# First three feed-forward elements issued inside the last steps of the first attention; two context loads issued earlier

## The chip, the cores and the metric

The kernel runs on one core of a Trainium2 chip. The metric is the device time of one execution in microseconds (us). The engines are called PE (TensorE, matmuls), DVE (VectorE), ACT (ScalarE), POOL (GpSimd) and SP (SyncE, which here issues most DMAs). Each takes its instructions strictly in the order in which they are written; semaphores make one wait for another.

## The reference

Two decoder layers over 16 batch elements, each of 128 rows by 128 columns (`x`), with a context of 120 rows per element.

```python
x = x + _L0_xattn_ref(_layernorm(x), ctx, ctx, Wq, Wk, Wv, Wo)        # 16 heads of 8, causal, softmax
x = x + _L0_ffn_ref(_layernorm(x), w_up, w_down)                       # 128 -> 512 -> gelu -> 128
x = x + _L1_xattn_ref(_layernorm(x), ctx, ctx, mask, Wq, ...)          # 16 heads of 64, relative positions
x = x + _L1_ffn_ref(_layernorm(x), rhs)                                # int8-like 128x128 product

# inside _L0_ffn_ref, for both weights:
alpha = jnp.mean(jnp.abs(w))
w_t = jnp.sign(w) * (jnp.abs(w) > 0.5 * alpha).astype(w.dtype)
rms = jnp.sqrt(jnp.sum(x * x, axis=-1, keepdims=True)) / jnp.sqrt(d)
x_norm = x / (rms + 1e-8)
```

## The kernel before, in words

The program has three stages, and in each the 16 elements pass one after the other through a software pipeline. `attn0(s, par)` is one step of the first attention, `ffn0(s, par)` one of the feed-forward part (FFN), `layer1(s, par)` one of the second layer. Each engine has its own version of the three functions. In step `s` an engine works on several elements at once: in `attn0(s)` the scores are those of element `s`, the scaling of the probabilities those of `s-1` and `s-2`, the product with the values that of `s-2`, and the residual sum `x_done` that of `s-3`. In `ffn0(s)` DVE takes the statistics of element `s+3` (`bn_stats`, `bn_aggr`, and a sum into `ve`) and normalizes `s+2` into `xn`; POOL takes the root of `s+3` (`rstd`, line 340); PE transposes `xn` of `s+1`, multiplies element `s` with `wup`, transposes the hidden values `hid` of `s-1` and multiplies `hidT` of `s-2` with `wdn`. ACT applies the gelu and copies the transposed values out of PSUM.

`run_steps` sets the order of the steps, the same for every engine: all of attention up to step 16, then `ffn0(-3)`, `attn0(17)`, `ffn0(-2)`, `attn0(18)`, `ffn0(-1)`, `attn0(19)`, and then the FFN from step 0. `attn0(19)` holds nothing. So the first FFN matmul stands behind the last attention matmul on PE. Element 15 is the last: from step 16 on attention has no new scores, and each step holds less.

PSUM has eight banks, `PS[:, 0..7, :]`. Attention keeps its scores in banks 0, 1, 3, 2 (head groups 0, 1, 2, 3), q, k and v in bank 4, the transposed probabilities in 4, 5 and 6, the transposed input in 6, and the outputs in 7. The FFN keeps the transposed input in banks 0 and 1, the `wup` products in 2 and 3, the transposed hidden values in 4 and 5, and the `wdn` products in 6 and 7. It may take a bank only when attention has finished with it; the waits on `A0["probs"]`, `A0["probT0"]` and so on in `ffn0` of PE say so. `probs` counts the exponentials of four head groups per element, so 61 to 64 are those of element 15.

Three small pieces of other work are spread over the attention steps: making `wup` and `wdn` ternary (POOL, lines 332 and 334, in steps 12 to 15), and rounding `rhsT` (DVE, lines 687 to 695), whose transposed form goes through PSUM bank 3 into `qrhs` and `rhs_scale` in step 17 (PE line 1111, DVE lines 743 and 744).

In the third stage `layer1(s)` on SP stores the relative-position products of element `s-1` and `s` (`store`, line 236), reads them back shifted (`shifted`, line 244), and loads context and mask of element `s` (lines 258 and 259). Those of element 0 are loaded in step 0, right after attention's last q, k, v product. Those of element 1 stand in step 1, behind `store(0, 1)` and `shifted(0, 0)`. On PE the key product of element 1 in step 1 waits for that context.

In the tables below a tile's name stands for several things: `relw` is also attention's expanded keys `kexp`, `relr` its second half of `probT0`. Line 964 is the helper `mm`, so it holds nearly all matmuls; line 980 transposes attention's probabilities, 1086, 1131 and 1329 transpose `xn` in the three stages, 1141 transposes `hid`.

## Time and profile before

| | |
|---|---|
| median of 3 runs | 462.59 us (461.73 to 464.74) |
| the profiled execution | 462.21 us |
| its span, first to last instruction | 460.4 us |
| mean granted clock of PE | 0.967 of full speed |
| busy: PE, DVE, ACT, POOL | 93%, 83%, 81%, 55% |

### The profile page before, as it was taken

Reading aid. Unit: us, or ns where it says so; the run is one execution under the profiler, and the core shown is the slowest. Engines: PE = TensorE matmul, PEld = TensorE weight load, DVE = VectorE, ACT = ScalarE, POOL = GpSimd, SP = SyncE. Lnnn points to the kernel's source line nnn. Section 1 sums busy time; section 2 is a strip of 40 time slices with the busy share of each in tenths; the row PEclk is TensorE's granted clock in tenths of the full one; section 3 lists DMA queues with packets and bytes.
Section 4 is the critical chain, followed back from the end, with each engine's and each line's share of the span. In section 5 each row is a group of like instructions: output and inputs, shape, how many; then the busy total and the mean of one; then the engine's idle time right before and its main releaser. Section 6 shows DMA issues by size and latency. Waiting matters only on the chain.

```text
span 460.4 us, 16745 instructions
## 1 busy us (share of the span) xinstructions
PE 428.4 (93%) x6147; PEld 317.8 (69%) x6147; DVE 384.3 (83%) x1316; ACT 370.7 (81%) x1467; POOL 252.8 (55%) x370
## 2 busy tenths in 40 slices
PE   8999999988779989799999999999999999999781
PEld 7556556555547768577887887888788778787570
DVE  5899999998468985489888989989898998988974
ACT  1999999989724564379899899899889989989961
POOL 4488888878935651023244444553654555355684
PEclk9999999999669999899999999999999999999987
DMA  7150000000000002777566565766746766476100
GB/s 216 51 192 22 14 12 6 10 7 8 1 2 1 0 2 69 190 193 186 127 160 150 126 165 123 161 147 140 180 108 159 155 144 163 120 180 148 29 7 23
DMA packets 54392, 44.88 MB, mean 97 GB/s; under 512 B 43952, under 2 KB 49328, under 8 KB 54320
## 3 DMA queue, kind: packets, MB, share of 16 engines
q1 hardware_dynamic: 53616, 43.59, 38.6%
q8 instruction: 46, 0.75, 0.7%
q10 hardware_dynamic: 704, 0.32, 0.2%
q14 instruction: 26, 0.21, 0.2%
HBM read 22.92 MB, written 20.97 MB: 95 GB/s over the span
## 4 chain that ended last, share of the span: by engine, by line
PE 78%; DVE 11%; ACT 4%; POOL 3%; DMA 1%; issue 1%; SPq 1%; POOLq 0%
PE PS L964 68%; PE PS L1161 4%; PE PS L980 2%; PE PS L1141 2%; POOL prob L307 1%; ACT prob L488 1%; DMA ctx<-in_ctxT 1%; DVE relw L709 1%; DVE nmax L666 1%; DVE nmax L668 1%; DVE relr L714 1%; PE PS L1086 1%; DVE nmax L640 1%; DVE qT L699 1%; DVE probT L647 1%
## 5 line engine op out<-in xcount | busy, mean ns | idle before, releaser
L351 POOL TENSOR_TENSOR prob<-prob,rsum 128x480 f32<-128x480 f32 x64 | 62.6, 989 | 70.7 <-DVE rsum L832 37.4
L488 ACT ACTIVATE prob<-prob,nmax 128x120 f32<-128x120 f32 x256 | 100.3, 414 | 0.0
L417 ACT ACTIVATE prob<-PS,nmax 128x120 f32<-128x120 f32 x256 | 89.4, 394 | 3.3 <-DVE nmax L731 2.9
L307 POOL TENSOR_TENSOR prob<-prob,rsum 128x480 f32<-128x480 f32 x64 | 62.5, 986 | 22.1 <-DVE rsum L704 12.4
L417 ACT ACTIVATION_READ_ACCUMULATOR prob<-PS,nmax 128x1 f32 x256 | 61.7, 241 | 0.0
L488 ACT ACTIVATION_READ_ACCUMULATOR prob<-prob,nmax 128x1 f32 x256 | 56.3, 220 | 0.0
L964 PE MATMUL PS<-rT,qv 64*32 64x152 f32 x2048 | 48.1, 297 | 2.4 <-ACT relw L567 2.4
L964 PE MATMUL PS<-ctx,wk 128*128 128x120 f32 x288 | 43.9, 289 | 2.3 <-DMA ctx<-in_ctxT 2.3
L964 PEld LDWEIGHTS PS<-xnT,wq 128*128 128x128 f32 x288 | 36.8, 191 | 9.3 <-issue 6.8
L964 PEld LDWEIGHTS PS<-rT,qv 64*32 64x32 f32 x2048 | 28.6, 106 | 20.6 <-issue 18.6
L964 PE MATMUL PS<-xnT,wq 128*128 128x128 f32 x288 | 42.5, 285 | 0.0
L964 PEld LDWEIGHTS PS<-ctx,wk 128*128 128x128 f32 x288 | 36.6, 195 | 7.1 <-issue 3.6
L964 PE MATMUL PS<-probT,hv 120*64 120x128 f32 x512 | 35.9, 284 | 3.3 <-ACT probT L595 3.3
L964 PE MATMUL PS<-wv,ctx 128*120 128x512 f32 (+1 forms) x96 | 39.0, 487 | 0.0
L964 PE MATMUL PS<-kT,qu 64*128 64x120 f32 x512 | 36.2, 281 | 0.0
L964 PE MATMUL PS<-relw,qT 32*128 32x480 f32 x128 | 34.4, 613 | 0.4 <-DVE relw L709 0.4
L964 PE MATMUL PS<-wo,oT_pairs 128*128 128x128 f32 x256 | 34.8, 280 | 0.0
L964 PEld LDWEIGHTS PS<-probT,hv 120*64 120x64 f32 x512 | 28.0, 139 | 7.9 <-ACT probT L595 3.7
L964 PEld LDWEIGHTS PS<-wo,oT_pairs 128*128 128x128 f32 x256 | 31.8, 195 | 1.8 <-ACT fin L502 0.8
L964 PEld LDWEIGHTS PS<-kT,qu 64*128 64x128 f32 x512 | 31.1, 188 | 2.5 <-issue 1.7
L980 PEld LDWEIGHTS PS<-ident,prob 64*120 64x120 f32 x512 | 18.9, 143 | 19.2 <-issue 19.2
L386 POOL TENSOR_TENSOR rstd_o<-ve_o,mhalf 128x1 f32<-128x1 f32 x16 | 13.1, 820 | 28.0 <-DVE ve_o L899 28.0
(195 smaller groups left out, 1100.6 us busy)
## 6 DMA issues: line engine op xcount, KB each, us to landing
rel_scratch<-relw SPq DMA_DIRECT2D x128, 152.0 KB, 2.7
relr<-rel_scratch SPq DMA_DIRECT2D x64, 240.0 KB, 4.3
ctx<-in_ctxT SPq DMA_DIRECT2D x32, 60.0 KB, 1.9
out_x<-fin SPq DMA_DIRECT2D x16, 64.0 KB, 2.2
x_all<-in_x SPq DMA_DIRECT2D x1, 640.0 KB, 7.1
wr<-in_wr SPq DMA_DIRECT2D x1, 512.0 KB, 5.0
wq<-in_wq SPq DMA_DIRECT2D x1, 512.0 KB, 3.7
wk<-in_wk SPq DMA_DIRECT2D x1, 512.0 KB, 4.5
```

Of the source, the lines that this page charges most:

```text
L307: return pool.tensor_tensor(pr, pr, cols(rsum[p], g, HG).unsqueeze(2).to_broadcast([S, HG, SK]), ALU.mult)
L351: return pool.tensor_tensor(pr, pr, cols(rsum[p], g, HG).unsqueeze(2).to_broadcast([S, HG, SK]), ALU.mult)
L386: pool.tensor_tensor(rstd2[p][:, :], ve2[p][:, :], mhalf[:, :], ALU.pow).then_inc(A1["orstd"], 1)
L417: last = act.activation(cols(prob[p], n, SK), cols(scores, q, SK), ACT.Exp, bias=nmax[p][:, n:n + 1], accum_out=ssum[p][:, n:n + 1])
L488: last = act.activation(cols(pr, n, SK), cols(pr, n, SK), ACT.Exp, bias=bias[:, n:n + 1], accum_out=total[:, n:n + 1])
L640: dve.tensor_reduce(out=cols(nmax[p], 2, HG), in_=heads(PS[:, 3, 0:HG * SK], HG), op=ALU.max, axis=AX.X, negate=True).then_inc(A0["nmax"], 1)
L647: dve.tensor_copy(query_half(probT0[0], 1), heads(PS[0:SK, 5, :], 2 * HG)).then_inc(A0["probT1"], 1)
L666: dve.tensor_reduce(out=cols(nmax[p], 0, HG), in_=heads(PS[:, 0, 0:HG * SK], HG), op=ALU.max, axis=AX.X, negate=True).then_inc(A0["nmax"], 1)
L964: return pe.matmul(o, a, b, start=start, stop=stop)
L980: last = pe.transpose(PS[0:SK, bank, q * S // 2:(q + 1) * S // 2], cols(prob[p], g * HG + q, SK)[rows], ident_sb[rows, rows])
L1141: last = pe.transpose(PS[:, 4 + p, c * S:(c + 1) * S], cols(hid[p], c, D), ident_sb[:, :])
L1161: last = pe.transpose(PS[0:SK, bank, q * S // 2:(q + 1) * S // 2], cols(prob[p], g * HG + q, SK)[rows], ident_sb[rows, rows])
```

## The change

Each engine gets a function `crossing()`, which writes out in what order it takes `attn0(14)` to `attn0(18)` and `ffn0(-3)` to `ffn0(2)`, and no longer the same for all. The last head group's and second head group's score banks change places (1 and 2), as do banks 5 and 6, through all of attention. The rounded `rhsT` passes through bank 7 in step 15, beside the output of element 12. POOL's last addition into `wdn` moves from step 15 to step 17. ACT loads the gelu table at the end of step 16. The FFN's waits for free banks follow the new numbers. Context and mask of elements 0 and 1 of the third stage are loaded one after the other as soon as attention's last q, k, v product is done.

```diff
@@ run_steps
-            peeled(attn0, LOOPS[0][1], NB + 1)
-            for s in range(3):
-                peeled(ffn0, s - 3, s - 2)
-                peeled(attn0, NB + 1 + s, NB + 2 + s)
-            peeled(ffn0, 0, LOOPS[1][0])
+            peeled(attn0, LOOPS[0][1], NB - 2)
+            crossing()
+            peeled(ffn0, 3, LOOPS[1][0])
@@ SP
+            def load_context(t, p):
+                at, mask_at = held(sp, t * SK), held(sp, t * S * SK)
+                sp.dma_start(ctx_sb[p][:, :], ctxT[:, bass.ds(at, SK)]).then_inc(A1[f"ctx_loaded{p}"], 16)
+                sp.dma_start(mask_sb[p][:, :], bass.AP(mask.tensor, mask_at, [[SK, S], [1, SK]]))\
+                    .then_inc(A1[f"mask_loaded{p}"], 16)
@@ SP layer1
-                    if isinstance(t, int) and t < 2:
-                        sp.wait_ge(A0["qkv_ps"], NB)
-                    after(sp, A1["hv_ps"], 2 * t - 2)
...
+                    if not (isinstance(t, int) and t < 2):
+                        sp.wait_ge(A1["hv_ps"], 2 * t - 2)
+                        load_context(t, p)
@@ SP ffn0
+                if at_step(s, -3):
+                    sp.wait_ge(A0["qkv_ps"], NB)
+                    for t in range(2):
+                        load_context(t, t)
@@ POOL
-                    if at_step(s, 13 + 2 * k):
+                    if at_step(s, 13 + 4 * k):
                         link(pool.tensor_tensor(w[:, :], w[:, :], change, ALU.add))
+            def crossing():
+                attn0(14, 0)
+                ffn0(-3, 1)
+                attn0(15, 1)
+                ffn0(-2, 0)
+                attn0(16, 0)
+                attn0(17, 1)
+                ffn0(-1, 1)
+                attn0(18, 0)
+                ffn0(0, 0)
+                ffn0(1, 1)
+                ffn0(2, 0)
@@ PE
+            def crossing():
+                attn0(14, 0)
+                attn0(15, 1)
+                ffn0(-3, 1)
+                ffn0(-2, 0)
+                ffn0(-1, 1)
+                attn0(16, 0)
+                ffn0(0, 0)
+                attn0(17, 1)
+                ffn0(1, 1)
+                attn0(18, 0)
+                ffn0(2, 0)
@@ DVE attn0, before the residual sum of element s - 3
+                    if at_step(s, NB - 1):
+                        link(dve.tensor_copy(qrhs[:, :], PS[:, 7, D:2 * D]))
+                        link(dve.tensor_copy(rhs_scale[:, :], PS[:, 7, 2 * D:3 * D]))
@@ PE attn0, before the output product of element s - 3
+                    if at_step(s, NB - 1):
+                        pe.wait_ge(setup_v, 17)
+                        pe.transpose(PS[:, 7, D:2 * D], qx[0][:, :], ident_sb[:, :]).then_inc(setup_p, 1)
+                        mm(PS[:, 7, 2 * D:3 * D], fin[0][:, :], ident_sb[:, :]).then_inc(setup_p, 1)
@@ PE ffn0, waits for free banks
-                        pe.wait_ge(A0["probs"], 63)
+                        pe.wait_ge(A0["probs"], 62)
                     if at_step(s, 1):
-                        pe.wait_ge(setup_v, 19)
+                        pe.wait_ge(A0["probs"], 64)
```

In the same notation the other two compute engines take their steps so. DVE: `ffn0(-3)`, `attn0(14)`, `attn0(15)`, `ffn0(-2)`, `attn0(16)`, `ffn0(-1)`, `attn0(17)`, `ffn0(0)`, `attn0(18)`, `ffn0(1)`, `ffn0(2)`. ACT: `attn0(14)`, `attn0(15)`, `attn0(16)`, `ffn0(-3)`, `ffn0(-2)`, `ffn0(-1)`, `attn0(17)`, `ffn0(0)`, `attn0(18)`, `ffn0(1)`, `ffn0(2)`. SP takes all five attention steps first.

PE before, from element 15's second product with the values (`relr,vexp`) to the third `wup` product:

```order
L964 MATMUL PS<-relr,vexp 32x128 x8
L1111 MATMUL PS<-ident,qx 128x128
L964 MATMUL PS<-ident,fin 128x128
L964 MATMUL PS<-wo,oT 128x128
L1131 MATMUL PS<-ident,xn 128x128
L964 MATMUL PS<-wup,xnT 128x512
L1131 MATMUL PS<-ident,xn 128x128
L964 MATMUL PS<-wup,xnT 128x512
L1131 MATMUL PS<-ident,xn 128x128
L1141 MATMUL PS<-ident,hid 128x128 x4
L964 MATMUL PS<-wup,xnT 128x512
```

Now, the same engine, from the first transposed probabilities of element 15 (line 1035 is 980 of before, 1019 is 964, 1185 is 1131, 1195 is 1141):

```order
L1035 MATMUL PS<-ident,prob 120x64 x16
L1019 MATMUL PS<-wup,xnT 128x512
L1185 MATMUL PS<-ident,xn 128x128
L1019 MATMUL PS<-wo,oT 128x128
L1035 MATMUL PS<-ident,prob 120x64 x16
L1019 MATMUL PS<-probT,vexp 32x128 x8
L1019 MATMUL PS<-relr,vexp 32x128 x8
L1019 MATMUL PS<-wup,xnT 128x512
L1185 MATMUL PS<-ident,xn 128x128
L1195 MATMUL PS<-ident,hid 128x128 x4
L1019 MATMUL PS<-wo,oT 128x128
L1019 MATMUL PS<-wup,xnT 128x512
```

The first `wup` product now stands before the second half of element 15's probabilities, the second one before the last attention product (`wo,oT`), and the two products for `rhsT` are gone from here.

POOL before, steps 15 to 17 and the FFN's first roots (`prob` rows are scalings, `vexp` spreads the values, `rstd` is the FFN's root):

```order
L315 TENSOR_TENSOR vexp<-v,vmask 120x512
L307 TENSOR_TENSOR prob<-prob,rsum 128x480 x3
L334 TENSOR_TENSOR wdn<-wdn,relw 128x512
L307 TENSOR_TENSOR prob<-prob,rsum 128x480
L315 TENSOR_TENSOR vexp<-v,vmask 120x512
L307 TENSOR_TENSOR prob<-prob,rsum 128x480 x3
L340 TENSOR_TENSOR rstd<-ve,half 128x2
L307 TENSOR_TENSOR prob<-prob,rsum 128x480
L340 TENSOR_TENSOR rstd<-ve,half 128x2 x3
```

POOL now, from the root of element 0 on:

```order
L357 TENSOR_TENSOR rstd<-ve,half 128x2
L324 TENSOR_TENSOR prob<-prob,rsum 128x480
L332 TENSOR_TENSOR vexp<-v,vmask 120x512
L324 TENSOR_TENSOR prob<-prob,rsum 128x480 x3
L357 TENSOR_TENSOR rstd<-ve,half 128x2
L324 TENSOR_TENSOR prob<-prob,rsum 128x480
L332 TENSOR_TENSOR vexp<-v,vmask 120x512
L324 TENSOR_TENSOR prob<-prob,rsum 128x480 x4
L351 TENSOR_TENSOR wdn<-wdn,relw 128x512
L357 TENSOR_TENSOR rstd<-ve,half 128x2 x2
```

Two roots have moved ahead of the last scalings, and the addition into `wdn` behind them.

SP before, at the start of the third stage:

```order
L258 DMA ctx<-in_ctxT 128x120
L259 DMA mask<-in_mask 128x120
L236 DMA rel_scratch<-relw 32x1216 x8
L244 DMA relr<-rel_scratch 64x8x120 x2
L258 DMA ctx<-in_ctxT 128x120
L259 DMA mask<-in_mask 128x120
L244 DMA relr<-rel_scratch 64x8x120 x2
```

SP now:

```order
L232 DMA ctx<-in_ctxT 128x120
L233 DMA mask<-in_mask 128x120
L232 DMA ctx<-in_ctxT 128x120
L233 DMA mask<-in_mask 128x120
L99 UNCONDITIONAL_BRANCH
L99 REGISTER_ALU
L99 COMPARE_AND_BRANCH
L253 DMA rel_scratch<-relw 32x1216 x8
L261 DMA relr<-rel_scratch 64x8x120 x4
```

The second context and mask stand ahead of all stores, and the four shifted reads follow one another.

## Rows read from the trace of the kernel before

**Rows 1.** Windows: busy time by engine, then granted clock (PEclk), DMA share, GB/s.
```profile
core 0: us, PE busy (x) PEld busy (x) DVE busy (x) ACT busy (x) POOL busy (x), PEclk, DMA share, GB/s
142.00:170.00 28.00, 28.00 (x186) 21.68 (x184) 24.82 (x137) 15.40 (x38) 16.57 (x22) 1.00 0.00 1
191.27:430.00 238.73, 237.05 (x4014) 189.09 (x4016) 211.19 (x655) 212.96 (x785) 109.98 (x176) 0.99 0.63 150
```

**Rows 2.** Timeline of PE over the crossing: start, length, what [idle before].
```profile
120.02 1.11 PE L980 MATMUL PS<-ident,prob 64*120 64x64 f32 x16 [1.89 <-POOL prob L307]
...
126.00 1.11 PE L980 MATMUL PS<-ident,prob 64*120 64x64 f32 x16 [0.92 <-POOL prob L307]
...
127.98 1.08 PE L964 MATMUL PS<-relr,vexp 120*32 120x128 f32 x16
...
131.60 0.30 PE L1131 MATMUL PS<-ident,xn 128*128 128x128 f32 x1 [1.48 <-DVE xn L770]
...
141.10 1.02 PE L964 MATMUL PS<-wup,xnT 128*128 128x512 f32 x2
141.96 0.27 PE L1131 MATMUL PS<-ident,xn 128*128 128x128 f32 x1
...
142.51 1.06 PE L964 MATMUL PS<-wdn,hidT 128*128 128x128 f32 x8
143.40 1.02 PE L964 MATMUL PS<-wup,xnT 128*128 128x512 f32 x2
```

**Rows 3.** Windows of half a microsecond in which the granted clock changes.
```profile
119.50:120.00 0.50, 0.00 (x0) 0.01 (x1) 0.14 (x1) 0.50 (x4) 0.50 (x2) 0.54 0.00 0
...
129.50:130.00 0.50, 0.50 (x4) 0.43 (x3) 0.07 (x1) 0.00 (x0) 0.00 (x0) 0.72 0.00 0
...
133.00:133.50 0.50, 0.50 (x3) 0.11 (x1) 0.41 (x3) 0.00 (x0) 0.01 (x1) 0.70 0.00 0
...
140.00:140.50 0.50, 0.50 (x6) 0.50 (x5) 0.32 (x1) 0.41 (x3) 0.40 (x1) 0.98 0.00 0
```

**Rows 4.** Timeline of POOL, steps 15 to 17.
```profile
117.54 1.27 POOL L334 TENSOR_TENSOR wdn<-wdn,relw 128x512 f32<-128x512 f32 x1
118.89 0.98 POOL L307 TENSOR_TENSOR prob<-prob,rsum 128x480 f32<-128x480 f32 x1
...
121.06 2.88 POOL L307 TENSOR_TENSOR prob<-prob,rsum 128x480 f32<-128x480 f32 x3
124.20 0.71 POOL L340 TENSOR_TENSOR rstd<-ve,half 128x2 f32<-128x2 f32 x1 [0.26 <-DVE ve L774]
```

**Rows 5.** Timeline of DVE: steps 14 and 15, then the FFN's first statistics.
```profile
105.79 0.66 DVE L666 TENSOR_REDUCE nmax<-PS 128x4 f32<-128x480 f32 x1 [0.62 <-PE PS L964]
...
117.08 0.29 DVE L740 COPY oT<-PS 128x128 f32<-128x128 f32 x1
...
123.35 0.28 DVE L759 BATCH_NORM_STATS2 stat<-x_all 128x6 f32<-128x128 f32 x1
...
123.89 0.23 DVE L774 TENSOR_SCALAR ve<-eps,mv 128x2 f32<-128x2 f32 x1
```

**Rows 6.** Timeline of DVE and POOL in the third stage, where two of them overlap.
```profile
210.49 1.93 POOL L351 TENSOR_TENSOR prob<-prob,rsum 128x480 f32<-128x480 f32 x2 [3.97 <-DVE rsum L832]
...
210.59 0.97 DVE L853 TENSOR_SCALAR xn<-x_all,mv,rstd 128x128 f32<-128x128 f32 x1
```

**Rows 7.** Timeline of SP, PE and DVE around the second context, third stage.
```profile
184.48 1.35 SPq L244 DMA_DIRECT2D relr<-rel_scratch  x2
185.88 0.62 SPq L258 DMA_DIRECT2D ctx<-in_ctxT  x1
...
191.27 2.06 PE L964 MATMUL PS<-ctx,wk 128*128 128x120 f32 x8 [2.30 <-DMA ctx<-in_ctxT]
191.56 0.65 DVE L920 TENSOR_TENSOR prob<-PS,relr 128x480 f32<-128x480 f32 x1
...
193.47 1.26 PE L964 MATMUL PS<-rT,qv 64*32 64x152 f32 x32
...
194.67 1.15 PE L964 MATMUL PS<-ctx,wk 128*128 128x120 f32 x8
```

125 lines of the change are left out of this document (74 added, 51 removed).

## The prediction

> **What bounds the kernel now.** I read the busy shares by stretch first, then PE's own timeline, then what it waits for. In the FFN, from 142 us on, PE is busy for 28.00 of 28.00 us, and in the third stage from 191.27 to 430 us for 237.05 of 238.73 us [rows 1]. In both, DVE, ACT and POOL have time left. So whatever brings PE earlier to one of these stretches should come out at the end in full, and nothing that only relieves another engine there counts. The places where PE is not the bound are the seams between the stages. At the first seam the last attention product with the values ends at 127.98 + 1.08 = 129.06 us, and the fourth `wup` product, from which the FFN runs in its regular step, starts at 141.10 [rows 2]. Those 12.04 us hold the two products for `rhsT`, one output product, an idle 1.48 us before the first transpose of the FFN [rows 2], and three FFN steps that begin from an empty pipeline. They also hold slow matmuls: the granted clock falls from 2.4 to 1.2 GHz at 119.5 us, after PE had waited 1.89 us for POOL [rows 2, 3], comes back at 129.8, falls again at 133.2 after the waits at the FFN's start, and is back at 140.0 [rows 3]. At the second seam, PE waits 2.30 us for the context of element 1 of the third stage and then runs its product at the low clock: 2.06 us against 1.15 for the same eight instructions at 194.67 [rows 7].
>
> **Part 1, the price: what the FFN's early pieces cost attention.** Ahead of step 14, DVE now takes the statistics of element 0. Before they last from 123.35 to 123.89 + 0.23, so 0.77 us [rows 5]. DVE has an idle 0.62 in that step, in which it waits for PE's scores [rows 5]; some 0.15 us is left over. POOL then has the root of element 0 before step 15: 0.71 us in its row [rows 4], 0.67 to the start of the next operation. POOL is busy without a gap there, so step 15 runs some 0.8 late on POOL, on the transposes that wait for it, and on DVE, where element 13's `oT` (117.08 to 117.37 before [rows 5]) ends at about 118.1. After it DVE has `ffn0(-2)`: den, statistics of element 1, `xn` of element 0, `ve`. From the statistics' 0.77 and the four operations between them I put this at 1.0 us, so `ve` is there at 119.1, and POOL's root of element 1 ends at 119.1 + 0.7 = 119.8. The scaling of element 14 that PE waits for begins then; before it began at 118.89 [rows 4]. The addition into `wdn`, 1.27 us ahead of it [rows 4], has gone from this place, and the net is still **0.9 us late**, since POOL now waits for DVE. From there POOL has the same sequence: one scaling, `vexp`, three scalings (to 121.06 + 2.88 = 123.94 before [rows 4]), now to 124.8. The last scaling of element 15 follows at once, where before the root at 124.20 [rows 4] stood between; it begins at 124.8, as late as before.
>
> On ACT the exponentials of element 15 that need DVE's last maximum come behind `ffn0(-2)`, some 1.3 us later than before. They are done by about 121.8, and POOL's scaling that needs them begins at 123.9: cover of 2 us. The gelu table load follows behind the copy of element 14's second half, and after it ACT has the transposed input of element 0 by 124.4. Nothing but the first `wup` product waits for it.
>
> PE, with its clock low as before: the second of POOL's three scalings ends two thirds into their 2.88 us, at 123.0 before [rows 4] and at 123.9 now, so the transposes of element 15's first half run from 124.0 to 125.1. Then comes the first `wup` product: 0.86 us at the high clock (141.10 to 141.96 [rows 2]), so some 1.8 at the low one, to 126.9. Transpose of element 1 and output product of element 14 reach 127.4, and the transposes that began at 126.00 before [rows 2] begin at 127.4. The last product with the values therefore ends at 127.4 + 3.06 = 130.4 us and not 129.06: the length 3.06 is that from 126.00 to 129.06. So the first piece of the FFN does delay attention's end, by **1.3 us**.
>
> **Part 1, the return.** What stands between that end and the fourth `wup` product is then: `wup` of element 1 (0.86), the transpose of `xn` and four of `hid` (141.96 to 142.51, 0.55), one output product (0.2, a quarter of the four products with `wdn`), `wup` of element 2 (0.86), 0.55 again, and the first product with `wdn` (142.51 to 143.40, 0.89) [rows 2]. That is 3.91 us at the high clock. To it I add 0.3 for ACT's copy that the third `wup` needs and 0.4 for DVE's `xn` of element 3, which stands behind the residual sum of element 15. Gelu of element 0 runs on ACT while PE is still in attention's last products. The fourth `wup` starts at 130.4 + 4.6 = 135.0 us, where before it started at 141.10: **6.1 us saved**. The clock is the large unknown in it. PE is now without a gap from about 124.0 on. Before, it took from 126.00 to 129.8 of gap-free work until the clock was back the first time, and the second time it came back at 140.0 [rows 2, 3], after a longer stretch of work. So I take it to be up by 130. If it comes up only where attention's end and half of the early FFN steps have passed, those 3.91 us double to at most 7.8, and 3.0 are left of the 6.1. If it never falls, because PE's wait for POOL is cut by the transpose of element 0, POOL's 124.8 is still the bound, PE's 3.06 and 1.8 us shrink by about a half, 2.4 together, and the saving is 8.5.
>
> The two products for `rhsT` and their DVE copies move to step 15. PE pays some 0.3 there, DVE 0.6 in front of a wait for PE like that of step 14; POOL, by then 0.8 late, hides both. The exchange of banks 1 and 2 and of 5 and 6 renames both sides of each wait, so I cost it at nothing from start to end of attention. The waits of the FFN for free banks ask for exponentials that are done by 121.8, before any of its `wup` products. The `wdn` addition ends at 127.0 on POOL, 7 us before its first use.
>
> **A rule that could add to the price.** In the trace, a normalization of DVE that takes its input and puts its output in SBUF begins just behind a POOL scaling and takes 0.97 us, until the first of the two POOL operations has ended [rows 6]. The Trainium skill, "SBUF — State Buffer", section "Who interferes with whom", says that VectorE and GpSimd share a pair of ports, which one takes for a whole instruction while the other stands still; by this rule the trace agrees. In the crossing DVE's `xn` of element 1 would meet a scaling of POOL at 124.8. It could last 0.97 us as well and end at 125.8, and PE needs it at 126.9, so it is covered. The `ve` of element 0 would meet POOL's addition into `wup` in step 14; were it held for most of such an addition (1.27 us in its row), step 14 would be some 0.7 us later on DVE, and the saving 5.4 instead of 6.1. The row of a `ve` at 123.89, begun under a scaling, has 0.23 us [rows 5, 4], so I take the price as nothing.
>
> **Part 2, the early context.** The wait of 2.30 us goes. What is late next: PE's key product of element 1 runs at 188.97 to 189.9, then a transpose to 190.2, and the relative products that follow ask for DVE's sum `added0` of element 0. That sum waits for the shifted read issued at 184.48, ahead of the context in SP's queue [rows 7], so it isn't earlier than before: 191.56 + 0.6 = 192.15 [rows 7]. Those products start at 192.15 and not at 193.47 [rows 7], 1.3 us earlier. At the high clock their end, 192.9, stands against 194.67 [rows 7]: 1.8 at most. If the clock falls again in the 1.95 us wait that is left, and comes back at the same place as before, the work that now runs ahead of the wait is worth about 0.7; if it falls later, nothing is left (0.1). PE's similar wait of 1.89 us was followed by a fall [rows 2, 3], so I take **0.7**, with 0 and 1.8 as ends. SP issues two DMAs fewer at 185.88, but the next shifted read waits for its stores.
>
> **The sum.** 462.21 - 6.1 - 0.7 = 455.4 us for the profiled execution. The median of the runs before is 0.4 above the profiled one, so I forecast **455.7 us**, 1.5% less. A measurement of this kernel can tell about 1% from no change.
>
> **The rivals.**
> 1. *The clock stays low through the early FFN.* Saving 3.0 + 0.1: 459.5. For it: PE's work from 124 on is interleaved with waits for four engines, and the clock took until 140.0 the second time. Against it: those waits are shorter than the ones before.
> 2. *The clock does not fall, or comes back before 127.* Saving 8.5 + 1.8: 452.3. For it: PE's longest wait has a transpose and a product in it. Against it: 1.5 us and more of it remain, and 1.89 were enough [rows 2].
> 3. *The overlap is mostly hidden.* The early FFN pieces lie in front of attention's on each in-order queue. If two of the three put PE a further 2 us behind, 6.1 becomes 2.1: 459.8 with part 2.
> 4. *Slower: a convoy.* Each engine mixes the steps in another order, so an FFN piece may wait for an attention piece of another engine that itself waits for an FFN piece. One such round trip, from DVE's statistics over POOL, DVE, PE and ACT to the `wup` product, takes about 3 us by the trace: 129.06 to 131.60 up to the transpose [rows 2], and a copy on ACT. With three of them, one per element, the end of attention would be 9 later: 462.6 + 9 - 6.8 = 464.8. It decides the sign once attention's last product ends after 137.2 us (130.4 + 6.8).
> 5. *The early context does nothing*, since the shifted read holds PE as long: 456.5. It lies within the forecast's range.
>
> **How the numbers follow.** Forecast, with either end of part 2 and 1.5 us of error in part 1: 0.66. Rival 2: 0.12. Rival 1: 0.10. Rival 3: 0.08. Rival 4: 0.04. The range is 451.8 to 459.9: it takes in rivals 2 and 1 nearly at their numbers, and leaves out rival 4 and the far halves of 2 and 3. Faster by over 1% means under 458.0: nearly all of the forecast and rival 2, 0.76. Within 1%: rivals 1 and 3 and a rest of the forecast, 0.20. Slower by over 1%: 0.04.
>
> **What the changed kernel's profile would show.** The POOL scaling of element 14 in step 16 begins near 119.8; attention's last product with the values ends near 130.4; the fourth `wup` starts near 135; between the two PE has no idle stretch over half a microsecond, and the granted clock is 1.00. The regular FFN step stays at 2.30 us (141.10 to 143.40 [rows 2]). In the third stage no wait for `ctx` is left, and one for `added0` of about 2 us stands in its place. The forecast is wrong if the last product ends much later than 131, if the clock falls again behind it, or if the third stage gives back what it got because DVE or the DMAs come as late as before.

## The result, and the profile after

| | before | changed kernel |
|---|---|---|
| median of the runs | 462.16 us (461.36 to 464.74, 4 runs) | 457.34 us (456.54 to 459.7, 4 runs) |
| profiled execution: time, span, granted clock | 462.21, 460.4, 0.967 | 456.54, 454.7, 0.985 |

The ratio is 0.9864, with a 95% interval of 0.9822 to 0.9906: faster by 1.4%, where 1.5% was forecast. Ratios leave out executions that a lower clock made over 1.5% longer than the fastest of their kernel; of the changed versions that is one (594.66 us at a clock of 0.653, experiment 9). Of the 5.7 us between the two profiled executions I account for each below. At the fourth `wup` product the changed kernel leads by 7.2 us, at the end of the FFN by 6.5, behind the second seam by 7.5, at the end by 5.7.

**The crossing.** The timeline of PE in the changed kernel, as [rows 2]:

```profile
117.43 0.64 PE L1019 MATMUL PS<-relr,vexp 120*32 120x128 f32 x16
...
121.22 0.68 PE L1035 MATMUL PS<-ident,prob 64*120 64x64 f32 x16 [1.28 <-POOL prob L324]
...
124.47 0.69 PE L1035 MATMUL PS<-ident,prob 64*120 64x64 f32 x16 [1.04 <-POOL prob L324]
125.08 1.13 PE L1019 MATMUL PS<-wup,xnT 128*128 128x512 f32 x2
...
128.38 0.64 PE L1019 MATMUL PS<-relr,vexp 120*32 120x128 f32 x16 [0.30 <-DVE relr L760]
128.96 1.12 PE L1019 MATMUL PS<-wup,xnT 128*128 128x512 f32 x2
...
133.91 1.02 PE L1019 MATMUL PS<-wup,xnT 128*128 128x512 f32 x2
```

The transposes of element 15's first half and the first `wup` stand behind one another at 124.47 and 125.08. The last product with the values begins at 128.38 and ends at 129.0, where it ended at 129.06 before. The fourth `wup` begins at 133.91 and not at 141.10. From the product at 117.43, which stands in attention's step 15, that is 16.48 us. The same product before is this row, and from it the way took 24.73 us:

```profile
116.37 0.65 PE L964 MATMUL PS<-relr,vexp 120*32 120x128 f32 x16
```

The 1.13 us of a `wup` is what it takes at the high clock (1.23 at 132.36 before), while before one took 2.05 to 2.07. The windows say the same: the granted clock is 1.00 from 117 to 142 us, in this window as in the others, where [rows 3] has 0.54 at 119.5.

```profile
122.00:124.00 2.00, 1.12 (x32) 0.61 (x24) 1.24 (x5) 1.97 (x5) 2.00 (x3) 1.00 0.03 8
```

The timeline of POOL answers to [rows 4], then three rows of DVE to [rows 5] and [rows 6]:

```profile
103.78 1.27 POOL L351 TENSOR_TENSOR wup<-wup,hsq 128x512 f32<-128x512 f32 x1
...
119.43 0.70 POOL L357 TENSOR_TENSOR rstd<-ve,half 128x2 f32<-128x2 f32 x1 [0.78 <-DVE ve L816]
120.09 0.99 POOL L324 TENSOR_TENSOR prob<-prob,rsum 128x480 f32<-128x480 f32 x1
...
122.27 3.83 POOL L324 TENSOR_TENSOR prob<-prob,rsum 128x480 f32<-128x480 f32 x4
```

```profile
104.32 0.77 DVE L816 TENSOR_SCALAR ve<-eps,mv 128x2 f32<-128x2 f32 x1
...
124.23 1.00 DVE L812 TENSOR_SCALAR xn<-x_all,mv,tiny 128x128 f32<-128x128 f32 x1
125.16 0.97 DVE L816 TENSOR_SCALAR ve<-eps,mv 128x2 f32<-128x2 f32 x1
```

The scaling of element 14 begins at 120.09, 1.2 us later than before. The `ve` of element 0 takes 0.77 us instead of 0.22 and ends at 105.09, within 0.04 us of POOL's addition into `wup` (103.78 + 1.27).

**The FFN.** PE is again busy for the whole of a window of 28 us, but compare the counts with [rows 1]: 181 matmuls, where there were 186.

```profile
134.50:162.50 28.00, 28.00 (x181) 20.76 (x180) 25.43 (x140) 15.44 (x37) 18.13 (x24) 1.00 0.00 0
```

```profile
143.16 1.02 PE L1019 MATMUL PS<-wup,xnT 128*128 128x512 f32 x2
144.18 0.33 PE L1185 MATMUL PS<-ident,xn 128*128 128x128 f32 x1
...
145.68 1.02 PE L1019 MATMUL PS<-wup,xnT 128*128 128x512 f32 x2
146.54 0.27 PE L1185 MATMUL PS<-ident,xn 128*128 128x128 f32 x1
...
147.98 1.02 PE L1019 MATMUL PS<-wup,xnT 128*128 128x512 f32 x2
```

A step takes 2.52 us (143.16 to 145.68), the next 2.30 (to 147.98), together 4.82. The loop's first pair of steps takes 4.65, the other three 4.80 to 4.82, where before each took 4.60: 0.67 us in all. In the long ones the transpose of `xn` begins 1.02 us behind `wup` instead of 0.86. What it waits for is DVE. In these rows of DVE, `xn` begins 0.27 us behind the small MEMSET ahead of it in one step and 0.07 in the next:

```profile
143.51 0.06 DVE L656 MEMSET gap<- 128x1 f32 x1
143.78 0.35 DVE L812 TENSOR_SCALAR xn<-x_all,mv,tiny 128x128 f32 x1
...
145.99 0.06 DVE L656 MEMSET gap<- 128x1 f32 x1
146.06 0.33 DVE L812 TENSOR_SCALAR xn<-x_all,mv,tiny 128x128 f32 x1
```

**The second seam.** The chain of waits (start, length, what), against [rows 7]:

```profile
177.96 0.65 SPq L261
...
178.66 6.37 DMA relr<-rel_scratch
...
185.78 0.58 DVE prob L975
...
186.49 9.14 PE PS L1019 x156
...
195.65 0.42 ACT relw L609
```

No wait for `ctx` is left, and the relative products wait for DVE's sums with the shifted read. From the first shifted read's issue to ACT's copy it takes 17.69 us; before it took 18.67 (184.48 to 203.15). The granted clock stays at 1.00 there, where before it was at 0.50 from 191.2 to 194.6. Experiment 2 asks whether the early context or the clock made the difference.

**The tail.** Windows of before, then of the changed kernel (PEclk is the third number from the end):

```profile
434.00:437.00 3.00, 1.32 (x27) 0.88 (x23) 2.89 (x11) 3.00 (x13) 2.58 (x6) 1.00 0.07 22
437.00:440.00 3.00, 2.80 (x20) 2.47 (x21) 2.84 (x10) 3.00 (x15) 2.52 (x4) 0.50 0.00 0
440.00:443.00 3.00, 2.96 (x37) 2.55 (x38) 2.22 (x12) 2.25 (x8) 2.61 (x5) 0.93 0.00 0
```

```profile
428.00:431.00 3.00, 1.47 (x17) 0.95 (x17) 2.93 (x9) 3.00 (x13) 2.17 (x4) 0.92 0.07 22
431.00:434.00 3.00, 2.55 (x18) 2.33 (x20) 2.76 (x13) 2.39 (x12) 2.61 (x6) 0.50 0.00 0
434.00:437.00 3.00, 3.00 (x25) 2.57 (x23) 0.74 (x6) 1.36 (x3) 2.92 (x6) 0.50 0.02 5
```

The clock falls in both, but for some 3.4 us before (437.0 to 440.4) and 6.8 in the changed kernel (430.5 to 437.3). From the same group of transposes (419.00 before, 411.50 after) to POOL's last sum (457.93 and 452.22) it takes 38.93 and 40.72 us:

```profile
419.00 0.68 PE L1161 MATMUL PS<-ident,prob 64*120 64x64 f32 x16
```

```profile
411.50 0.68 PE L1229 MATMUL PS<-ident,prob 64*120 64x64 f32 x16
```

That is the 1.8 us by which the lead shrinks at the end.

### The profile page after: what moved, and what is told of

The parts are those of the page before. It is cut to its first block, busy times and chain, and to the rows that moved or that the text cites. A ratio compares the mean times of both kernels' runs of the same rounds, so it can differ in the third digit from the quotient of the medians.

```text
span 454.7 us, 16744 instructions
## 1 busy us (share of the span) xinstructions
PE 422.3 (93%) x6147; PEld 313.4 (69%) x6147; DVE 385.8 (85%) x1316; ACT 371.5 (82%) x1467; POOL 253.9 (56%) x370
## 4 chain that ended last, share of the span: by engine, by line
PE 77%; DVE 13%; ACT 4%; POOL 2%; DMA 1%; issue 1%; SPq 0%; POOLq 0%; DVEq 0%
PE PS L1019 67%; PE PS L1229 4%; PE PS L1035 3%; ACT prob L531 2%; PE PS L1195 1%; DMA relr<-rel_scratch 1%; DVE relr L760 1%; DVE nmax L712 1%; DVE nmax L714 1%; DVE relw L755 1%; POOL prob L324 1%; DVE nmax L683 1%; DVE probT L690 1%; PE PS L1145 1%; DVE nmax L777 1%
## 5 line engine op out<-in xcount | busy, mean ns | idle before, releaser
L1019 PE MATMUL PS<-ctx,wk 128*128 128x120 f32 x288 | 42.9, 285 | 0.0
L1019 PE MATMUL PS<-wo,oT_pairs 128*128 128x128 f32 x256 | 36.0, 287 | 0.5 <-ACT fin L545 0.5
L1019 PEld LDWEIGHTS PS<-wo,oT_pairs 128*128 128x128 f32 x256 | 32.8, 200 | 2.4 <-ACT fin L545 1.3
L1035 PEld LDWEIGHTS PS<-ident,prob 64*120 64x120 f32 x512 | 17.8, 135 | 19.0 <-issue 19.0
```

The source lines that it names most:

```text
L1019: return pe.matmul(o, a, b, start=start, stop=stop)
L1035: last = pe.transpose(PS[0:SK, bank, q * S // 2:(q + 1) * S // 2], cols(prob[p], g * HG + q, SK)[rows], ident_sb[rows, rows])
```

## The experiments

Each was timed beside the kernel before on its chip; ratios are to it. The stretches of all profiled executions first, since most verdicts rest on them. **Crossing** is from the start of the product with the values in attention's step 15 to the start of the fourth `wup`; **FFN** from there to SP's first shifted read. PEclk says whether the granted clock fell between 117 and 133 us. "Kept busy" stands for constant products on PE, "one read first" for a changed order of two DMAs; both are explained below.

| kernel | crossing | PEclk | FFN | time us (median) | ratio [95%] |
|---|---|---|---|---|---|
| before | 24.73 | falls | 43.38 | | |
| changed | 16.48 | 1.00 | 44.05 | 457.34 | 0.9864 [0.9822, 0.9906] |
| changed, again | 16.48 | 1.00 | 44.06 | 458.19 | 0.9857 [0.9806, 0.9909] |
| crossing alone | 18.22 | falls | 44.05 | 458.45 | 0.9859 [0.9810, 0.9907] |
| context alone | 24.60 | falls | 43.38 | 464.68 | 0.9994 [0.9959, 1.0029] |
| FFN unrolled | 18.23 | falls | 43.38 | 459.99 | 0.9895 [0.9839, 0.9952] |
| before, kept busy | 21.33 | 1.00 | 43.86 | 458.91 | 0.9897 [0.9840, 0.9953] |
| `wdn` addition in step 15 | 18.94 | falls | 44.06 | 458.85 | 0.9906 [0.9870, 0.9943] |
| one read first | 18.03 | falls | 44.05 | 456.39 | 0.9863 [0.9810, 0.9915] |
| third stage kept busy | 17.86 | falls | 44.04 | 456.37 | 0.9849 [0.9804, 0.9894] |
| `wup` addition in step 12 | 16.46 | 1.00 | 44.06 | 461.50 | 0.9932 [0.9892, 0.9971] |
| kept busy, FFN unrolled | 16.47 | 1.00 | 43.39 | 455.57 | 0.9822 [0.9770, 0.9874] |
| the same, again | 16.48 | 1.00 | 43.37 | 454.35 | 0.9778 [0.9730, 0.9827] |
| the same, one read first | 16.47 | 1.00 | 43.38 | 456.41 | 0.9809 [0.9753, 0.9865] |

The rest of the same executions: **third stage** from the first shifted read to the group of transposes with which the tail begins (419.00 before), with whether the clock fell at the second seam; **tail** from there to POOL's last sum, with how long the clock was low in its first low stretch. A later one, up to the end, they all have.

| kernel | contexts | third stage | clock at the seam | tail | low in it |
|---|---|---|---|---|---|
| before | late | 234.52 | falls | 38.93 | 3.4 |
| before, kept busy | late | 232.67 | 1.00 | 39.00 | 3.4 |
| crossing alone | late | 234.25 | falls | 40.73 | 6.8 |
| context alone | early | 234.52 | falls | 39.58 | 3.4 |
| changed | early | 233.54 | 1.00 | 40.72 | 6.8 |
| changed, again | early | 232.90 | 1.00 | 39.51 | 3.4 |
| FFN unrolled | early | 234.86 | falls | 41.36 | 6.8 |
| `wdn` addition in step 15 | early | 232.53 | 1.00 | 39.72 | 3.4 |
| one read first | early | 232.85 | 1.00 | 39.60 | 3.4 |
| third stage kept busy | early | 233.18 | 1.00 | 39.27 | 0 |
| `wup` addition in step 12 | early | 235.47 | falls | 39.59 | 3.4 |
| kept busy, FFN unrolled | early | 233.14 | 1.00 | 39.48 | 0 |
| the same, again | early | 233.53 | 1.00 | 39.45 | 0 |
| the same, one read first | early | 235.28 | falls | 39.25 | 0 |

**1. The crossing alone.** The changed kernel with only element 0's context loaded early:

```
-                    if not (isinstance(t, int) and t < 2):
-                        sp.wait_ge(A1["hv_ps"], 2 * t - 2)
+                    if not (isinstance(t, int) and t < 1):
+                        after(sp, A1["hv_ps"], 2 * t - 2)
                         load_context(t, p)
...
-                    for t in range(2):
-                        load_context(t, t)
+                    load_context(0, 0)
```

> The changed kernel without its second part: the context of element 1 of the third stage is again loaded in step 1, behind the shifted read. Theory (the two parts add up): the fourth wup product starts at about 134 us as in the changed kernel (133.9 there, 141.1 before), PE waits for the context again (about 2.3 us), and the time is 0.5 to 1 us above the changed kernel's, 4.5 to 6 below before. Rival (the early context gives nothing, since the shifted read holds PE as long): the time is that of the changed kernel.

The time is that of the changed kernel within the intervals: 0.9859 against 0.9864. PE waits 1.28 us at 122.16 as in the changed kernel, but here the clock falls behind that wait:

```profile
122.00:124.00 2.00, 1.54 (x40) 1.26 (x44) 0.95 (x3) 1.98 (x9) 2.00 (x3) 0.83 0.04 8
128.00:130.00 2.00, 2.00 (x20) 1.46 (x18) 0.29 (x1) 0.00 (x0) 0.95 (x2) 0.50 0.00 0
```

So one and the same order of instructions in the crossing has two outcomes, 16.48 us and 18.22. Of the eight profiled executions with this crossing and no added products in it (two of them with one of POOL's additions in another step), the clock stayed up in three.

**2. The context alone.** The kernel before with the first two contexts loaded early, nothing else.

```
...
             def ffn0(s, par):
-                pass
+                if at_step(s, -3):
+                    sp.wait_ge(A0["qkv_ps"], NB)
+                    for t in range(2):
+                        load_context(t, t)
```

> The kernel before with the early contexts alone. Theory: the crossing is as before (fourth wup at about 141), no wait for the context, a wait of PE for DVE's sum in its place, the relative products 1.0 us earlier than before counted from the end of the FFN, time 0.5 to 1.5 us under before. The shifted read of element 0 lands 0.5 us or more later after its issue than before (5.2 us from the end of its issue before, 5.8 in the changed kernel), since the next one is now issued right behind it. Rival (the later landing in the changed kernel has another cause, such as the shift of everything by 7 us): it lands as before, and the gain is 1.5 us or more.

No difference can be measured (0.9994). In the trace the stretch of relative and key products begins 7.84 us after the first shifted read's issue (186.84 to 194.68) instead of 9.06 (184.48 to 193.54). This is 1.2 us earlier, but it is not what the lost wait gives: with the late contexts, and PE's waits for them of 2.02 and 0.88 us still there, the same stretch begins 7.87 us after the issue in experiment 1 (180.64 to 188.51) and 7.72 in experiment 4, whose chain of waits has

```profile
188.61 1.15 PE PS L964 x8
...
189.87 9.08 PE PS L964 x156
```

The 9.06 were those of one execution, in which the context came late and its product ran at the low clock (2.06 us instead of 1.15). In experiment 2 the clock falls at 196.0, and the whole third stage takes 234.52 us, as before. The second table sorts by the clock and not by the contexts: where it stayed up at the seam, 232.67 us with late contexts and 232.53 to 233.54 with early ones; where it fell, 234.25 and 234.52 with late, 234.52 to 235.47 with early. No gain from the early contexts shows, neither in the time nor in a trace, though late contexts at the high clock were profiled only once.

**3. The FFN unrolled.** The changed kernel with the eight looped FFN steps written out:

```
             peeled(ffn0, 3, LOOPS[1][0])
-            looped(ffn0, LOOPS[1])
-            peeled(ffn0, LOOPS[1][1], NB - 1)
+            peeled(ffn0, LOOPS[1][0], NB - 1)
```

> The changed kernel with its FFN written out from step 4 to 14 instead of a loop over pairs of steps. In the changed kernel the steps of the loop take 2.40 us and not 2.30, and the lead of 7.2 us at the fourth wup is 6.5 at the end of the FFN. Theory (DVE with the loop's extra instructions needs 4.80 us for a pair, and is now the bound, since it no longer has the head start it had before): the steps take 2.30 us, the lead stays 7.1 to 7.2, the time is about 0.6 us under the changed kernel. Rival (DVE needs 2.4 us for a step with or without the loop, because of its port shared with POOL): nothing changes.

```profile
135.39 1.02 PE L1018 MATMUL PS<-wup,xnT 128*128 128x512 f32 x2
...
137.69 1.02 PE L1018 MATMUL PS<-wup,xnT 128*128 128x512 f32 x2
```

Every step takes 2.30 us, and the FFN stretch 43.38 instead of 44.05. So in the traces the looped form costs 0.67 us once PE has no slack ahead of it; the runs that have the loop written out (here and in experiment 9) all take 43.37 to 43.39, the others with this crossing 44.04 to 44.06. The loop was unrolled on every engine, and that DVE's part is what counts is read from the rows above. The time doesn't show the gain (0.9895): in the profiled execution the clock fell at the crossing, at the second seam and in the tail, and against the changed kernel's execution the crossing takes 1.75 us more, the third stage 1.32 and the tail 0.64.

**4. The kernel before, kept busy.** Nineteen constant products on PE in the waits of the old crossing, results unused:

```
+                    if isinstance(s, int) and s >= NB:
+                        pe.wait_ge(A0["probs"], 61)
+                        for _ in range({16: 7, 17: 3, 18: 6}[s]):
+                            mm(PS[:, 0, 0:D], mean_w[:, :], mean_w[:, :])
...
+                    if at_step(s, 0):
+                        pe.wait_ge(setup_v, 19)
+                        for _ in range(3):
+                            mm(PS[:, 3, 0:D], mean_w[:, :], mean_w[:, :])
```

> The kernel before with 19 products of a constant on PE, whose results nobody reads, in its idle stretches between 118 and 135 us: 7 in step 16, 3 in step 17, 6 in step 18, 3 behind the first wup product. It computes all that before does. Theory (a good part of the crossing's saving is the clock, which no longer falls): the granted clock stays at 1.00 from 117 to 142, and the fourth wup starts about 3 to 4.5 us earlier than 141.1, at 137 or so, the time 3 to 4 under before. Rival (the saving is overlap, and the clock has little part in it): the fourth wup is earlier by under 1.5 us though the clock stays up. If the clock falls all the same, this tells nothing about either.

```profile
128.01 0.64 PE L964 MATMUL PS<-relr,vexp 120*32 120x128 f32 x16 [0.30 <-DVE relr L714]
...
131.61 1.10 PE L964 MATMUL PS<-wup,xnT 128*128 128x512 f32 x2 [0.46 <-ACT xnT L472]
...
138.29 1.02 PE L964 MATMUL PS<-wup,xnT 128*128 128x512 f32 x2
```

The old order at a clock of 1.00 has the fourth `wup` at 138.29 us, 2.8 earlier than [rows 2], and the time falls by 1.0%. This splits the gain. At the high clock the crossing takes 21.33 us in the old order and 16.48 in the new: 4.85 us are overlap. At a clock that falls it is 24.73 against 17.86 to 18.23: 6.5 to 6.9. The low clock costs the old order 3.4 us and the new one 1.4 to 1.75. A small part of the 21.33 is the added products' own: `xn` of element 1 is ready at 132.53, and its transpose begins at 133.21, behind the three products that follow the first `wup`. So, as an estimate from these rows, the overlap is worth up to 0.6 us less than 4.85 and the clock as much more. What in the new order gave it (the FFN's early pieces, the banks, the moved `rhsT`) no run separates, but for the `wdn` addition of experiment 5.

The time is a warning: 0.9897 [0.9840, 0.9953] can't be told from the 0.9864 of the changed kernel or the 0.9859 of experiment 1. Nineteen added products gave nearly as much as the whole new order. In this execution the clock also stayed up at the second seam, which before it did not.

**5. The `wdn` addition back in step 15.** `13 + 4 * k` becomes `13 + 2 * k` in the changed kernel.

> The changed kernel with one edit: GpSimd's addition into wdn stands in step 15 again instead of step 17. Theory (GpSimd's chain of scalings sets when the last probabilities are transposed, and with them everything up to the fourth product with wup): GpSimd is idle for 0.78 us ahead of the root at 119.43, and the addition takes 1.35, so the last scaling of element 14 and the transposes behind it come about 0.6 us later (transposes at 121.8 instead of 121.22, last product with values at about 129.0 instead of 128.38). In exchange nothing of 1.35 us stands ahead of the third element's root, which may give up to 0.3 back at the wait of 0.34 ahead of the transpose at 132.41: the fourth product with wup at 133.9 to 134.6, time 0 to +0.6 us against the changed kernel, ratio to before about 0.987. Rival (the vector engine sets the crossing, GpSimd only waits for it): the transposes stay at 121.2 and nothing moves. Rival 2 (a later start leaves TensorE idle longer, 1.9 instead of 1.28 us, and its clock falls there): the fourth product at 136 to 137, time +2 to +3.

```profile
118.80 1.26 POOL L351 TENSOR_TENSOR wdn<-wdn,relw 128x512 f32<-128x512 f32 x1
...
121.11 0.98 POOL L324 TENSOR_TENSOR prob<-prob,rsum 128x480 f32<-128x480 f32 x1
```

The crossing is 0.7 to 1.1 us longer than in the others whose clock fell. The theory said 0.6 for the start of the transposes (they begin at 122.24, 4.61 after the product with the values, against 3.79 in the changed kernel: 0.8), and a part back at the third root, of which nothing shows. Moving this addition was worth some 0.8 us in the trace; the time (0.9906 [0.9870, 0.9943]) can't be told from the changed kernel's.

**6. One read first.** In the changed kernel, SP issues element 0's second shifted read when the first has landed:

```
                     sp.wait_ge(A1["stored1"], 64 * t + 64)
+                    if at_step(t, 0):
+                        sp.wait_ge(A1["relr00"], 32)
                     shifted(t, p, 1)
```

> The changed kernel, in which SyncE issues the second shifted read of element 0's relative scores only when the first has landed. In the changed kernel all four reads are issued within 4.2 us from 177.96 on and the one waited for lands at 185.1, 7.2 us after the issue began; before it was 6.5. Theory A (reads issued back to back share the DMA engines, and the early contexts, by letting SyncE issue them sooner, made the first one slower): the first read lands about 0.5 to 0.7 us earlier (6.5 after the issue of the first), the second some 2 to 4 us later, and the wait of the relative products moves to the second: ahead of the next softmax step ACT's copies come up to 2 us later unless they have that slack. Time -0.5 to +2 us against the changed kernel. Theory B (the landing is the DMA's own latency of some 6.4 us from the issue, whatever else is queued): first read unchanged, second later, time 0 to +2 us.

The chain has `180.46 4.92` for the landing, 5.6 us after the issue began at 179.77. Without the edit, it is 6.1 to 7.3 us in nine executions where four reads are issued in a row. This agrees with theory A's first half and doesn't show it: the changed kernel alone has 7.1 and 6.4 in its two executions, and in experiment 9 a read issued alone took 6.0. The next context then waits in SP's queue until 194.22 and PE for it until 198.26. The time is 456.39: no loss, and no gain that the intervals can tell.

**7. Third stage kept busy.** The changed kernel with constant products in waits of the third stage:

```
+                    if at_step(s, NB + 2):
+                        keep_busy(1, 2)
...
+                    if at_step(s, NB + 2):
+                        keep_busy(7, 3)
...
+                    if at_step(t, 1):
+                        keep_busy(3, 10)
                     after(pe, A1["added0"], t)
...
+                    if isinstance(s, int) and s >= NB + 1:
+                        keep_busy(1, 4)
                     pe.wait_ge(A1["probT3"], t + 1)
```

> The changed kernel with constant products on TensorE in idle time of the third stage alone: ten ahead of the wait for the relative scores at 183.7 to 186.5, and in steps 17 and 18 four ahead of the last product with values, two and three ahead of the output product and the dequantising product of step 18. Their results are not used. Theory (the lead of 7.5 us at 411.57 shrank to 5.7 at the end because the granted clock fell at 430.8 for 6.4 us in the changed kernel and at 437.0 for 3.2 us before it): with the clock at 1.00 from 425 to 438 the stretch from the transposes at 411.57 to the end takes about 2 us less (43.1 us now), and the whole about 455 us, ratio to before 0.981 to 0.984; at the second seam nothing changes where the clock did not fall (up to 1.5 us in the executions where it did). Rival (the tail is set by the chain ScalarE-VectorE of the last softmax and dequantisation, where TensorE's speed is hidden): clock 1.00 there but the stretch from 411.57 to the end stays 43 us, time unchanged. Rival 2 (the products themselves delay the waits they stand ahead of by more than they give): +0.5 us or more.

```profile
431.00:434.00 3.00, 2.35 (x32) 1.98 (x30) 2.79 (x11) 3.00 (x16) 2.61 (x6) 1.00 0.02 5
434.00:437.00 3.00, 2.96 (x52) 2.50 (x49) 1.97 (x13) 1.76 (x6) 2.61 (x5) 1.00 0.00 0
```

The clock is 1.00 up to 443, and the tail takes 39.27 us (412.21 to 451.48) instead of 40.72. Of the 2 us expected, 1.45 came. But most of it comes without the products too: in the changed kernel's other profiled execution (experiment 9) the clock was low for 3.4 us there and not 6.8, and the tail took 39.51. The two products ahead of the output product stand behind the wait there (they start at 432.16, when it has ended) and hold it up by 0.55 themselves: a small share of rival 2. All six runs lie between 455.8 and 458.1.

**8. The `wup` addition in step 12.** `13 + 4 * k` becomes `12 + 5 * k`: a test of what held the `ve` of element 0.

> The changed kernel with GpSimd's addition into wup in step 12 instead of step 13. Theory (the variance row of FFN element 0 takes 0.77 us on the vector engine instead of 0.2 because GpSimd's addition runs over it, and this delays every later step of the attention by 0.5): that row takes 0.20 to 0.25, the span from the copy of oT ahead of it to the copy of oT(13) falls from 14.57 to about 14.0, and the time by 0.5 us. Rival (GpSimd then works 1.27 us longer ahead of step 13's scalings, which the transposes wait for): the row is short but oT(13) comes no earlier, or up to 1.3 us later; time 0 to +1.3. Rival 2 (the row is long for a reason of its own, such as its operands): it stays at 0.77.

```profile
97.15 1.26 POOL L351 TENSOR_TENSOR wup<-wup,hsq 128x512 f32<-128x512 f32 x1
...
106.59 1.27 POOL L332 TENSOR_TENSOR vexp<-v,vmask 120x512 f32<-120x512 f32 x1 [1.26 <-PE PS L1019]
```

```profile
99.62 0.69 PE L1035 MATMUL PS<-ident,prob 64*120 64x64 f32 x16 [2.02 <-POOL prob L324]
```

```profile
107.30 0.59 DVE L816 TENSOR_SCALAR ve<-eps,mv 128x2 f32<-128x2 f32 x1
```

My theory's cure was worse than the harm. PE waits 2.02 us for POOL at 99.62, its clock falls and is low from 100.8 to 114.5, and attention reaches step 15's product with the values at 122.23 instead of 117.43. The row itself speaks for the mechanism all the same: `ve` now meets another POOL operation, `vexp`, and ends with it (107.89 and 107.86), taking 0.59 instead of 0.77. So it is as long as what is left of POOL's operation. What the 0.5 us are worth to the whole wasn't measured.

**9. Kept busy, and the FFN unrolled.** Experiments 7 and 3 together, and four constant products in each of the two waits for POOL in step 16:

```
+                    if at_step(s, NB):
+                        keep_busy(5, 4)
                     pe.wait_ge(A0["probT1"], free)
...
                     freed(pe, (A0["v"], free, t + 2), (A0["probT0"], t, t - 1))
+                    if at_step(s, NB):
+                        keep_busy(4, 4)
```

> The kernel before it in this list, with two more edits: constant products in the two stretches of 1.28 and 1.04 us where TensorE waits for GpSimd's scalings in step 16 of the crossing (four each), and the eight FFN steps of the loop written out one after another instead of looped. Theory: the clock stays at 1.00 through the crossing in every execution (the fourth product with wup at 133.9 in the profile, where the runs with a low clock had 135.4 and 136.6), each FFN step takes 2.30 us instead of 2.40 (0.7 us over the stage), and the third stage as in the kernel before it. Together about 454 us in the median, ratio to before 0.977 to 0.982, with less spread between executions than the changed kernel. Rival (written-out steps cost as much in fetched code as the loop cost on the vector engine): FFN steps of 2.30 in the trace but no gain beyond 455. Rival 2 (the clock falls elsewhere as soon as it is held in one place): the low stretches come back at other places and the time is 456 to 457, as the changed kernel.

Five of its six executions lie between 454.05 and 456.46 us. The crossing takes 16.47 and the FFN 43.39. The rerun beside the changed kernel:

> The kernel with the clock held and the FFN unrolled again, beside the changed kernel and the one with one read first. Theory: median 454 to 456, below the changed kernel by 1.5 to 2.5 us, ratio to before 0.979 to 0.983. Rival (its lead over the changed kernel came from executions with a lucky clock): within 1 us of the changed kernel.

It gave 454.35 us, with all six between 454.15 and 454.94, where the changed kernel's six lie between 454.64 and 459.1:

> The changed kernel as it stands, so that it is timed beside the others on one chip. Expected 456.5 to 458, ratio to before 0.984 to 0.988. In the trace the stretch from the value product of step 15 to the fourth product with wup takes 16.5 us if the granted clock stays at 1.00 there and 18.0 to 18.3 if it falls; the stretch from there to the first shifted read takes 44.05 either way.

So in this set the version does every time what the changed kernel did at its best; in the first set it did so in three of these five. The medians differ by 3.8 us, where 1.5 to 2.5 were expected. Its interval, 0.973 to 0.983, is the lowest of the study. With one read first on top:

> The kernel with the clock held and the FFN unrolled, with the edit of the one read first on top: SyncE issues element 0's second shifted read when the first has landed. Theory (a read issued alone lands 5.6 us after its issue began, one with three more behind it 6.1 to 7.2, and the relative products wait for the first only): the first read lands at most 5.7 us after its issue began, and the third group of relative copies comes 0.5 to 0.7 us earlier; the time is 0.3 to 0.7 us under that of the kernel without the edit, which runs again beside it. Rival (that landing differs by as much from execution to execution, and the second read becomes the one waited for): the same time within 0.3 us.

The median was 456.41 (0.9809), no gain, and the six lie between 454.33 and 458.73: the steadiness is gone. The first read lands 6.0 us after its issue began, but PE then waits 0.79 for the next context, and in the profiled execution the clock fell behind that wait (199.7 to 203.1). This execution was also some 2.6 us late before the crossing began (120.06 against 117.33 to 117.55), with the clock low between 21 and 29 us, so not all of its 458.73 belongs to the edit. The expected 5.7 was missed, the gain was absent.

## Why the prediction was right, and where it was wrong

**The time** (455.7 forecast, 457.34 measured, within the range) came out near, and some of that is luck. Part 1 gave about 1 us more than forecast because the clock happened to stay up, part 2 was credited with 0.7 us that no run shows, and two losses for which the sum had no term (the FFN's loop and the tail) took away 2.5.

**Part 1, the price.** `ve` of element 1 was put as done at 119.1; it begins at 119.12 and ends at 119.34. The scaling of element 14 was put at 119.8 and begins at 120.09, which is 1.2 late instead of 0.9. I put the extra down to the port rule that I weighed and priced at nothing; no run took the hold away, so its price is argued. The `ve` of element 0 took 0.77 us while POOL's addition ran, and experiment 8 shows its length follow POOL's operation. By the Trainium skill, "SBUF — State Buffer", section "Who interferes with whom", one of the two stands still for the other's whole instruction; the trace agrees with it here. My row against it was the wrong witness: that `ve` of 0.23 began at 123.89, 0.05 us before the scaling ended at 123.94 [rows 4, 5], so there was nothing left to hold it. In the changed kernel `xn` at 124.23 and `ve` at 125.16 took 1.00 and 0.97, both under scalings. As forecast, these two were covered.

**Part 1, the clock.** The step "PE, with its clock low as before" failed in the profiled execution: the clock never fell, which is rival 2's condition, with 0.12 as its chance, and came in three of eight executions. With it the last product ended at 129.0 and not 130.4, and the fourth `wup` came at 133.91 and not 135.0. The sum itself was good: in the four variants with this order whose clock fell in the profiled execution (experiments 1, 3, 6, 7) it came at 134.99 to 136.59. Rival 2's bonus of 2.4 us was too large: the low clock costs the new order 1.4 to 1.75. What was wrong was to give the two clocks fixed chances for the kernel, when they are two outcomes of executions.

**"Whatever brings PE earlier to one of these stretches should come out at the end in full"** was the step that failed on substance, together with "the regular FFN step stays at 2.30". Busy for 28.00 of 28.00 hid that DVE's looped step took as long: before, DVE takes 2.33 and 2.49 us for two steps in turn, 4.82 for PE's 4.60:

```profile
146.51 0.21 DVE L752 TENSOR_SCALAR tiny<-rstd 128x1 f32<-128x1 f32 x1
...
148.84 0.21 DVE L752 TENSOR_SCALAR tiny<-rstd 128x1 f32<-128x1 f32 x1
...
151.33 0.21 DVE L752 TENSOR_SCALAR tiny<-rstd 128x1 f32<-128x1 f32 x1
```

It drew on a head start from PE's late start: its `xn` of element 4 was done at 139.49, and PE took it at 141.96. In the changed kernel it is done at 134.56 and taken at 134.77, and from 143.16 on PE followed DVE, a pair of steps in 4.80 to 4.82. Experiment 3 gives the 0.67 us back, and in experiment 4, where PE came 2.8 us earlier in the old order, half a microsecond of it is lost already (43.86).

**Part 2** was put at 0.7 with 0 and 1.8 as ends; the two profiled executions differ by 0.98, and that is not its return. In the runs it comes out at the lower end, as rival 5 had it: alone it is 0.9994 [0.9959, 1.0029], experiment 1 without it is level with the changed kernel, and the third stage is as long with late contexts as with early ones once the clock did the same (experiment 2). The step that failed is that the products would start 1.3 us earlier, at 7.67 us after the shifted read's issue. They started 8.53 after it in the changed kernel and 7.88 in its other execution, while the late contexts reached 7.72 and 7.87 (experiments 4 and 1). There too DVE's sum was done only 7.52 and 7.43 us after the issue, so the wait for the context hid next to nothing but that sum. The price of 1.3 us was read from one execution, with its 9.06 (experiment 2). The `added0` wait was forecast as about 2 us and is 2.85 in one execution of the changed kernel and 2.21 in the other; in the first the shifted read took 0.64 us longer to land, for a reason that isn't shown.

**The tail** had no term in my sum. The 1.8 us lost there go with how long the clock is low there, and I find no edit that they belong to: executions with the new crossing have 3.4 us and 6.8, those with the old one, of which there are three, 3.4. With constant products it isn't, and the tail is 1.45 shorter (experiment 7); with 3.4 us of low clock instead of 6.8 the same kernel's is 1.21 shorter. In sum: 7.19 - 0.67 + 0.98 - 1.79 = 5.71 us of 5.67 measured. This adds up two executions and not the edits: the last two terms are different in the changed kernel's other one.

Rivals 3 and 4 didn't occur: attention's end moved by less than 0.1 us (129.06 to 129.02), and to 130.11 to 130.84 in experiments 3, 6 and 7, at the low clock for which 130.4 was forecast, and no engine waited in a round. What stays open is why the clock falls in one execution and not in another with the same waits; no run here varied only that.

## What to carry to other kernels

A stretch in which one engine shows 100% busy isn't proof that only this engine bounds it: look at what the next engine takes per step, and at the count of instructions in the window, before you carry a lead through it. When you close a gap on TensorE, work out the sum at both granted clocks, and ask of every other wait whether the clock falls there. Before you credit an edit with a stretch that got shorter, look for another execution with the same clock there: here 1 us at a seam belonged to the clock. Try the cheap rival first: a few products with unused results inside the waits (and not behind them) gave most of the time in the old order. In the new one they went with less spread, 0.8 and 2.4 us between executions instead of 4.5, but 4.4 where one read more had been held back.

## What the runs showed of the hardware

- The same order of instructions with the same wait of 1.28 us on PE stayed at a granted clock of 1.00 behind it in some executions and fell to 0.50 for 6.8 us in others ("changed, again" and experiment 1).
- A DVE operation of 0.22 us on 128x2 elements took 0.59, 0.77 and 0.97 us when a POOL operation ran beside it, and ended within 0.04 us of that operation. Not every DVE operation is held: one on 128x1 elements at 123.69 took 0.21 us inside the scalings that run from 122.27 to 126.10.
- In the looped FFN, DVE's two steps took 2.33 and 2.49 us; written out, each took 2.27 (144.22 to 146.49). Most of the difference lies ahead of the operations on a row of `x_all`; why is not tested.
- A shifted read alone in SP's queue landed 5.6 and 6.0 us after its issue began (two executions), one with three more behind it 6.1 to 7.3 (nine); one and the same kernel had 6.4 and 7.1.
- In the tail, a low clock for 6.8 us went with 40.72 to 41.36 us, one for 3.4 with 38.93 to 39.72, none with 39.25 to 39.48.
